# Rotary products taken straight from PSUM and added on GpSimd, one tile per step

## The chip, the core and the metric

The kernel runs on one core of one Trainium2 chip. The metric is the device time of one execution in microseconds. Five engines work side by side, each with its own instruction queue that it works off in order: TensorE (PE in the profile), VectorE (DVE), ScalarE (ACT), GpSimd (POOL) and SyncE (SP), which here only issues DMAs. They meet through semaphores.

## The reference, cut to what matters

Four sequences of 1024 tokens of width 128 go through causal attention with 8 heads of width 128, a layer norm, a gated feed-forward network and another layer norm, all in float32. What the change touches is the rotation of queries and keys:

```python
even, odd = jnp.split(x, 2, axis=-1)
return jnp.concatenate([even * cos - odd * sin, even * sin + odd * cos], axis=-1)
...
s = jnp.einsum('bihd,bjhd->bhij', q, k) / D_HEAD
s = s - INF_APPROX * mask          # mask is 1 where i < j
p = jax.nn.softmax(s, axis=-1)
```

## The kernel before, in words

Attention runs as 32 heads (4 sequences of 8), in pairs, in a loop whose body is written out. Matrix products are made from float32 numbers split into a high and a low float32r part, three products each (high by high, high by low, low by high). Head by head the work is a pipeline of eight steps, s = 0 to 7, one for each block of 128 query rows. In step s of the running head

- TensorE makes the scores of block s + 2 (blocks 0 and 1 of the next head in steps 6 and 7), then transposes the probabilities of block s, then projects tiles of the queries and keys of the next head, then values (in steps 4, 5, 6, 6 of the first head of a pair only), then pieces of the product of probabilities and values. Each is a call in `step` of the TensorE block, and nothing overtakes.
- VectorE takes the reciprocal of the row sums of block s + 1 (`inverse_sum`), the maximum of the scores of block s + 2 (`negative_max`), adds a head to the residual (steps 0 and 4), makes the low part of the transposed block s, and does its part of the rotation.
- ScalarE takes the exponential of block s + 1, makes the high part of a rotated tile, the high part of the transposed block, and in the kernel before the copy `proj`.
- GpSimd multiplies the probabilities of block s + 1 by the reciprocal sums (`normalize`, L720), then does its part of the rotation: `times_sin` (L725) and the low part `roped_low` (L732).

I write *norm(n)* for GpSimd's normalization of block n, *scores(n)* for TensorE's product of block n, and *low(j)* for `roped_low` of tile j.

A head has four tiles to rotate: 0 and 1 are the first 512 tokens of the queries and of the keys, 2 and 3 the second 512. The rotation needs the two halves of the 128 dimensions exchanged; that is a pair of DMAs from one SBUF tile to another, issued by SyncE. Before the change a tile goes through: projection (TensorE, into a PSUM bank), copy to `proj` (ScalarE), swap DMA, product with the sine (GpSimd, from SBUF), product with the cosine (VectorE, from PSUM), sum (VectorE), high part (ScalarE), low part (GpSimd). The tuples `QK_STEP` to `LOW_STEP` at the top say in which step of the running head each tile takes each of these; 8 means step 0 of the head after. Within a step each engine does them in the order in which its `step` function calls them.

What waits for the rotation is `scores`: it holds for

```python
wait_for(pe, rope_low, head, 1 if ib < 4 else 3)
```

so scores(0) of a head wait for low(1), and scores(4), in step 2 of the head itself, wait for low(3).

`plan_banks` gives PSUM banks to scores, transposes, projections and values by least recent use; it reads `QK_STEP`. The causal mask is added to the scores by a product of an identity and a 128x128 triangle, both bf16 before, between the first and second product of the diagonal half (L393).

Of the kernel before, what the change touches and what calls it, by code (L numbers as in the profile page):

```python
# [17 lines left out]
F32R = mybir.dt.float32r  # L18
# [9 lines left out]
P = 128  # L28
# [18 lines left out]
ROPE_TILES = [(0, 0), (1, 0), (0, 1), (1, 1)]  # L47


QK_STEP = (0, 0, 2, 2)  # L50
COS_STEP = (0, 0, 2, 2)
SIN_STEP = (1, 2, 3, 4)
SUM_STEP = (2, 3, 4, 6)
HIGH_STEP = (3, 4, 6, 8)
LOW_STEP = (3, 4, 6, 8)
V_STEP = (4, 5, 6, 6)
PV0_PIECES = {6: range(0, 2), 7: range(2, 4)}
PV1_PIECES = {1: range(0, 2), 2: range(2, 4), 3: range(4, 8)}
# [61 lines left out]
def attention(nc, ctx, sem, rT, ident, x_split, qk_split, v_split, xT, w_q, w_k, w_vT, w_o, rope_in, ident_in, mask_in,  # L120
# [3 lines left out]
        return where.enter_context(nc.sbuf_tensor(name, shape, dt))  # L124

    rope = sb("rope", [P, 2, T])
    ident_b = sb("ident_b", [P, P], BF16)
    mask_b = sb("mask_b", [P, P], BF16)
    w_stage = sb("w_stage", [P, 2, 4, P], F32R)
    wv_stage = sb("wv_stage", [P, 2, 2 * P], F32R)  # L130
    x_moving = sb("x_moving", [P, 2, 2, T], F32R)
    qk = sb("qk", [P, 2, 2, 2, T], F32R)
    proj = sb("proj", [P, 2, BANK])
    by_cos = sb("by_cos", [P, NQK, BANK])
    swapped = sb("swapped", [P, NQK, BANK])

# [43 lines left out]
    t_high = (sem("t_high"), NT)  # L180
    t_low = (sem("t_low"), NT)
    qk_projected = (sem("qk_projected"), NQK)
    proj_copied = (sem("proj_copied"), 4)
    cos_done = (sem("cos_done"), 4)
    sin_done = (sem("sin_done"), 4)
    rope_done = (sem("rope_done"), 4)
# [26 lines left out]
    def step_on(head, by):  # L213
        return head[0], head[1] + by
# [99 lines left out]
    with nc.Block() as block:  # L314
        @block.sync
        def _(sp):

            sp.dma_start(raw_w[:, 0], w_q).then_inc(qk_loaded, 16)
            sp.dma_start(raw_w[:, 1], w_k).then_inc(qk_loaded, 16)
            sp.dma_start(rope[:], rope_in).then_inc(consts_loaded, 16)  # L320
            sp.dma_start(mask_f[:], mask_in).then_inc(consts_loaded, 16)
            sp.dma_start(ident[:], ident_in).then_inc(consts_loaded, 16)
            for b in range(1, B):
                sp.dma_start(raw_x[:, b], xT[:, b * T:(b + 1) * T]).then_inc(x_loaded[b], 16)


            def stage_x_moving(b):

                wait_for_pair(sp, v_projected, PAIRS_OF * (b - 1) - 1, NV - 1)
                sp.dma_start(x_moving[:, b % 2].bitcast(F32), x_split[b - 2]).then_inc(x_moved, 16)  # L330

            def stage_pair(b, hp):

                pair = PAIRS_OF * b + hp
                dynamic = not isinstance(hp, int)
                first = isinstance(pair, int) and pair == 0

                def stage_for_values():
                    src = v_parts[:, :, :2 * P].bitcast(F32) if first else v_split[hp] if not dynamic else \
                        v_split[bass.ds(sp.snap(hp + 0), 1)].rearrange("o p k d -> p (o k) d")  # L340
                    wait_for_pair(sp, v_projected, pair - 1, NV - 1)
                    if first:
                        sp.wait_ge(vo_low, 1)
                    sp.dma_start(wv_stage[:].bitcast(F32), src).then_inc(wv_staged, 16)

                for q in range(2):
                    head = (pair, q)
                    src = qk_split[bass.ds(sp.snap(2 * hp + q), 1)].rearrange("o p k d -> p (o k) d") if dynamic else \
                        qk_split[2 * hp + q]
                    if not first:  # L350
                        wait_for(sp, qk_projected, step_on(head, -2), NQK - 1)
                        sp.dma_start(w_stage[:, q].bitcast(F32), src).then_inc(w_staged[q][0], 16)
                    if q == 0 and not first:
                        stage_for_values()
                    for j in range(NQK):
                        wait_for(sp, proj_copied, head, j)
                        for lo, hi in ((0, 64), (64, 0)):
                            sp.dma_start(swapped[lo:lo + 64, j], proj[hi:hi + 64, j % 2]).then_inc(
                                swap_done[j % 2][0], 16)
                    if q == 0 and first:  # L360
                        stage_for_values()

            stage_pair(0, 0)
            sp.wait_ge(w_saved, W_SAVED)
            with sp.Fori(1, PAIRS_OF) as hp:
                stage_pair(0, hp)
            sp.wait_ge(x_saved, X_SAVED)
            for base, src in zip(FFN_AT, ffn_weights):
                sp.dma_start(ffn_raw[:, base:base + src.shape[1]], src).then_inc(ffn_loaded, 16)
            for b in range(1, B):  # L370
                stage_pair(b, 0)
                if b < B - 1:
                    stage_x_moving(b + 1)
                with sp.Fori(1, PAIRS_OF) as hp:
                    stage_pair(b, hp)

        @block.tensor
        def _(pe):
            def scores(head, ib):
# [7 lines left out]
                for h in range(halves):  # L387
                    dst = score_ps[:, ib % 2, h, :half]
                    left = [a[:, ib * P:(ib + 1) * P] for a in q]
                    right = [a[:, h * half:(h + 1) * half] for a in k]  # L390
                    nc.tensor.matmul(dst, left[0], right[0], start=True, stop=False)  # L391
                    if h == halves - 1:
                        nc.tensor.matmul(dst[:, half - P:], ident_b[:], mask_b[:], start=False, stop=False)  # L393
                    nc.tensor.matmul(dst, left[0], right[1], start=False, stop=False)  # L394
                    last = nc.tensor.matmul(dst, left[1], right[0], start=False, stop=True)  # L395
                last.then_inc(scores_ready[0], 1)
# [86 lines left out]
        def _(act):  # L483
# [55 lines left out]
                        bank("t", head[1], nth)[:, :n_blocks * P].rearrange("p (j i) -> p j i", i=P),  # L539
                        ACT.Copy).then_inc(t_high[0], 1)  # L540

            def copy_projected(head, j):
                wait_for(act, qk_projected, head, j)
                old_head, old = earlier(head, j, 2, 4)
                wait_for_swap(act, old_head, old)
                wait_for(act, rope_low, step_on(head, -1), j)

                nc.scalar.activation(proj[:, j % 2], bank("qk", 1 if parity(head) else 2, j),  # L548
                                     ACT.Copy).then_inc(proj_copied[0], 1)

            def roped_high(head, j):
                which, c = ROPE_TILES[j]
                wait_for(act, rope_done, head, j)
# [12 lines left out]
            def step(head, s, b):  # L566
# [25 lines left out]
                for target, j in rope_tasks(head, s, QK_STEP):  # L592
                    copy_projected(target, j)
                for c in v_tasks(head, s):
                    values_high(head[0], c)

# [3 lines left out]
        def _(dve):  # L600
# [45 lines left out]
                        low, bank("t", head[1], nth)[:, :n_blocks * P].rearrange("p (j i) -> p j i", i=P),  # L646
                        high.bitcast(F32), ALU.subtract).then_inc(t_low[0], 1)

            def times_cos(head, j):
                c = ROPE_TILES[j][1]  # L650
                wait_for(dve, proj_copied, head, j)
                wait_for(dve, rope_done, step_on(head, -1), j)
                nc.vector.tensor_tensor(by_cos[:, j], bank("qk", 1 if parity(head) else 2, j),
                                        rope[:, 0, c * BANK:(c + 1) * BANK],
                                        ALU.mult).then_inc(cos_done[0], 1)

            def rope_sum(head, j):
                wait_for(dve, sin_done, head, j)
                wait_for(dve, cos_done, head, j)
                nc.vector.tensor_tensor(swapped[:, j], by_cos[:, j], swapped[:, j], ALU.add).then_inc(rope_done[0], 1)  # L660
# [19 lines left out]
            def step(head, s, b):  # L680
                if before_first(head) and s == 3:
                    dve.wait_ge(vo_high, 1)
                    nc.vector.tensor_tensor(v_parts[:, 1], vo_ps, v_parts[:, 0].bitcast(F32),
                                            ALU.subtract).then_inc(vo_low, 1)
                    nc.vector.tensor_copy(ident_b[:], ident[:])
                    nc.vector.tensor_copy(mask_b[:], mask_f[:]).then_inc(masks_ready, 1)
                if before_first(head) and s == 5:
                    for b in range(1, B):
                        low_of_x(b)
                if exists(step_on(head, (s + 1) // NI)):  # L690
                    inverse_sum(step_on(head, (s + 1) // NI), (s + 1) % NI)
                for target, j in rope_tasks(head, s, SUM_STEP):
                    rope_sum(target, j)
                if exists(step_on(head, (s + 2) // NI)):
                    negative_max(step_on(head, (s + 2) // NI), (s + 2) % NI)
                if s == ADD0_STEP:
# [2 lines left out]
                    add_head(step_on(head, -1), 1)  # L699
                if exists(head):  # L700
                    transposed_low(head, s)
                for target, j in rope_tasks(head, s, COS_STEP):
                    times_cos(target, j)
                for c in v_tasks(head, s):
                    values_low(head[0], c)

# [3 lines left out]
        def _(pool):  # L710
# [8 lines left out]
                p = probs[:, ib % 4, :(ib + 1) * P]  # L719
                nc.gpsimd.tensor_scalar(p, p, inv_sum[:, n:n + 1], 1.0, ALU.mult, ALU.mult).then_inc(probs_ready[0], 1)  # L720

            def times_sin(head, j):
                c = ROPE_TILES[j][1]
                wait_for_swap(pool, head, j)
                nc.gpsimd.tensor_tensor(swapped[:, j], swapped[:, j], rope[:, 1, c * BANK:(c + 1) * BANK],  # L725
                                        ALU.mult).then_inc(sin_done[0], 1)

            def roped_low(head, j):
                which, c = ROPE_TILES[j]
# [4 lines left out]
            def step(head, s, b):  # L734
                ahead = step_on(head, (s + 1) // NI)
                if exists(ahead):
                    normalize(ahead, (s + 1) % NI)
                for target, j in rope_tasks(head, s, SIN_STEP):
                    times_sin(target, j)
                for target, j in rope_tasks(head, s, LOW_STEP):  # L740
                    roped_low(target, j)

# [459 lines left out]
```

## Time and profile before

| | us |
|---|---|
| median of 3 runs (1081.2 to 1084.93) | 1084.09 |
| the profiled execution's own time | 1084.27 |
| its span | 1082.5 |
| TensorE busy | 1000.0 |
| VectorE busy | 852.7 |
| ScalarE busy | 657.0 |
| GpSimd busy | 584.8 |

Attention fills the span up to about 785 us, the feed-forward part the rest. The start of scores(0) of one head and of the next lie 22.83 to 25.01 us apart. In the trace a head can be recognised by its scores: the L391 product is 128 columns wide for block 0, 256, 384 and 512 for blocks 1 to 3, and twice 320, 384, 448 and 512 for blocks 4 to 7. In the stretch used below, the head that is running up to 407.95 us is the second of its pair (it projects no values), and the one running from there to 430.78 us is the first of the next pair (it does).

### The profile page before, as it was taken

To read this page: it belongs to the slowest core of one execution; us is meant where nothing else is said; L and a number is where in the kernel's file an instruction comes from. 1 tells how busy PE (TensorE), PEld (TensorE's weight loads), DVE (VectorE), ACT (ScalarE), POOL (GpSimd) and SP (SyncE) were. 2 spreads that over 40 slices of the span, in tenths; PEclk is the share of its full clock that TensorE was granted. 3 is DMA by queue.
4 is the path that set the end of the run, shared out by engine and by line. 5 is a ranking of instruction groups with operands and counts; after the bars stand their busy time and mean duration, and the time that the engine had idled before them with its cause. 6 is when DMAs were issued, how large, how long until landed. Compare 5 with 4: busy or idle time off the path is not lost. (4 is left out here: it accounts for less than half of the span.)

```text
span 1082.5 us, 20027 instructions
## 1 busy us (share of the span) xinstructions
PE 1000.0 (92%) x5648; PEld 829.6 (77%) x5648; DVE 852.7 (79%) x1803; ACT 657.0 (61%) x1383; POOL 584.8 (54%) x536
## 2 busy tenths in 40 slices
PE   2799999999999999999999999999929999999995
PEld 1588788878878888887888888787727878788784
DVE  4888888988878898897989888888755668486744
ACT  4577776777767777776767777677625252343531
POOL 3676777777767777777787776778450101000000
PEclk8899999999999999999999999999969999999998
DMA  7542223532222323222222223231020000000000
GB/s 247 166 137 60 63 63 87 156 88 59 59 60 67 78 58 88 59 61 67 68 67 58 50 59 73 59 80 42 1 79 1 1 1 21 0 19 0 1 20 20
DMA packets 33292, 66.16 MB, mean 61 GB/s; under 512 B 5456, under 2 KB 6992, under 8 KB 32208
## 3 DMA queue, kind: packets, MB, share of 16 engines
q1 hardware_dynamic: 30400, 58.62, 20.4%
q10 hardware_dynamic: 2832, 6.82, 1.7%
q8 instruction: 29, 0.48, 0.2%
q14 instruction: 31, 0.25, 0.1%
HBM read 24.26 MB, written 7.34 MB: 29 GB/s over the span
## 5 line engine op out<-in xcount | busy, mean ns | idle before, releaser
L720 POOL TENSOR_SCALAR probs<-probs,inv_sum 128x128 f32<-128x128 f32 (+7 forms) x256 | 236.2, 923 | 177.9 <-DVE inv_sum L635 177.9
L537 ACT ACTIVATE pT<-psum 128x512 fp32r<-128x512 f32 (+3 forms) x384 | 176.1, 490 | 129.8 <-PE psum L404 128.7
L311 PE MATMUL psum<-pT,vals 128*128 128x512 f32 (+3 forms) x1152 | 243.5, 351 | 1.6 <-DVE rT L678 1.6
L525 ACT ACTIVATE probs<-psum,neg_max 128x128 f32<-128x128 f32 (+7 forms) x256 | 190.5, 744 | 57.3 <-DVE neg_max L629 55.6
L645 DVE TENSOR_TENSOR pT<-psum,pT 128x512 fp32r<-128x512 f32 (+3 forms) x384 | 199.9, 547 | 15.1 <-ACT pT L537 12.0
L311 PEld LDWEIGHTS psum<-pT,vals 128*128 128x128 f32 x1152 | 188.9, 190 | 23.6 <-DVE pT L645 1.7
L629 DVE TENSOR_REDUCE neg_max<-psum 128x1 f32<-128x128 f32 (+7 forms) x256 | 190.4, 744 | 6.3 <-PE psum L395 6.3
L404 PE MATMUL psum<-ident,probs 128*128 128x128 f32 x1152 | 175.8, 278 | 15.0 <-POOL probs L720 7.6
L725 POOL TENSOR_TENSOR swapped<-swapped,rope 128x512 f32<-128x512 f32 x128 | 166.2, 1299 | 39.5 <-DMA swapped<-proj 38.6
L901 PE MATMUL ps<-hid,w 128*128 128x512 f32 x768 | 181.3, 396 | 0.0
L901 PEld LDWEIGHTS ps<-hid,w 128*128 128x128 f32 x768 | 143.7, 188 | 34.5
L732 POOL TENSOR_TENSOR qk<-swapped,qk 128x512 fp32r<-128x512 f32 x128 | 166.1, 1298 | 2.8 <-ACT qk L556 2.8
L404 PEld LDWEIGHTS psum<-ident,probs 128*128 128x128 f32 x1152 | 134.5, 141 | 42.1 <-DVE pT L645 13.1
L391 PE MATMUL psum<-qk 128*128 128x384 f32 (+5 forms) x384 | 136.7, 356 | 25.8 <-POOL qk L732 22.9
L660 DVE TENSOR_TENSOR swapped<-by_cos,swapped 128x512 f32<-128x512 f32 x128 | 123.1, 963 | 44.9 <-POOL swapped L725 44.9
L394 PE MATMUL psum<-qk 128*128 128x384 f32 (+5 forms) x384 | 151.3, 394 | 0.0
L395 PE MATMUL psum<-qk 128*128 128x384 f32 (+5 forms) x384 | 131.8, 343 | 0.0
L311 PE MATMUL psum<-x_moving,w_stage 128*128 128x512 f32 (+1 forms) x384 | 106.7, 414 | 9.9 <-DVEq L622 9.9
L995 ACT ACTIVATE value<-ps,scales 128x512 f32<-128x512 f32 x64 | 43.5, 690 | 96.9 <-PE ps L901 96.5
L391 PEld LDWEIGHTS psum<-qk 128*128 128x128 f32 x384 | 73.0, 190 | 36.0 <-issue 26.8
L1026 POOL COPY y<-y_norm 128x512 f32<-128x512 f32 (+1 forms) x8 | 5.2, 653 | 166.3 <-DVE y_norm L1083 166.3
L548 ACT ACTIVATE proj<-psum 128x512 f32<-128x512 f32 x128 | 75.2, 600 | 30.8 <-PE psum L311 26.1
(78 smaller groups left out, 1246.5 us busy)
## 6 DMA issues: line engine op xcount, KB each, us to landing
swapped<-proj SPq DMA_DIRECT2D x256, 128.0 KB, 2.3
w_stage<-qk_split SPq DMA_DIRECT2D x30, 256.0 KB, 2.7
wv_stage<-v_split SPq DMA_DIRECT2D x15, 256.0 KB, 2.6
x_split<-ffn_raw ACTq DMA_DIRECT2D x2, 1024.0 KB, 5.9
ffn_raw<-g SPq DMA_DIRECT2D x2, 1024.0 KB, 8.2
x_moving<-x_split SPq DMA_DIRECT2D x2, 1024.0 KB, 6.0
out<-y SPq DMA_DIRECT2D x4, 512.0 KB, 2.6
raw_x<-xT SPq DMA_DIRECT2D x3, 512.0 KB, 11.5
```

Source lines behind the costliest of these rows:

```text
L311: ins = nc.tensor.matmul(out_ap, left[a], right[b], start=first and i == 0, stop=last and i == 2)
L391: nc.tensor.matmul(dst, left[0], right[0], start=True, stop=False)
L394: nc.tensor.matmul(dst, left[0], right[1], start=False, stop=False)
L404: last = nc.tensor.transpose(bank("t", head[1], nth)[:, (jb % 4) * P:(jb % 4 + 1) * P], probs[:, ib % 4, jb * P:(jb + 1) * P], ident[:])
L525: nc.scalar.activation(probs[:, ib % 4, :width].rearrange("p (h c) -> p h c", h=halves), score_ps[:, ib % 2, :halves, :half], ACT.Exp, bia ...
L537: nc.scalar.activation(pT[chunk][:, 0, 4 * f:4 * f + n_blocks, (ib % 4) * P:(ib % 4 + 1) * P], bank("t", head[1], nth)[:, :n_blocks * P].r ...
L629: nc.vector.tensor_reduce(neg_max[:, n:n + 1], score_ps[:, ib % 2, :halves, :half], AX.XY, ALU.max, negate=True).then_inc(max_ready[0], 1)
L645: nc.vector.tensor_tensor(low, bank("t", head[1], nth)[:, :n_blocks * P].rearrange("p (j i) -> p j i", i=P), high.bitcast(F32), ALU.subtra ...
L720: nc.gpsimd.tensor_scalar(p, p, inv_sum[:, n:n + 1], 1.0, ALU.mult, ALU.mult).then_inc(probs_ready[0], 1)
L725: nc.gpsimd.tensor_tensor(swapped[:, j], swapped[:, j], rope[:, 1, c * BANK:(c + 1) * BANK], ALU.mult).then_inc(sin_done[0], 1)
L732: nc.gpsimd.tensor_tensor(low, swapped[:, j], high.bitcast(F32), ALU.subtract).then_inc(rope_low[0], 1)
L901: last = nc.tensor.matmul(ps[:, c, o], w_at(base, a, k * HID, o * P), hid[:, c, layer, b, k], start=k == 0 and i == 0, stop=k == HT - 1 an ...
```

## The change

The sine product moves from GpSimd, after the swap, to VectorE, before the swap, and reads the projection in PSUM; the copy on ScalarE is gone. The swap DMA carries the sine product instead of the projection, so the sine table changes its signs. GpSimd adds the two products in place of multiplying. Tiles are projected one per step, and the tuples move: tile j is projected in step j; low(0) to low(3) come in steps 4, 5, 8 and 9 instead of 3, 4, 6 and 8. Identity and mask become float32r.

```diff
-QK_STEP = (0, 0, 2, 2)
-COS_STEP = (0, 0, 2, 2)
-SIN_STEP = (1, 2, 3, 4)
-SUM_STEP = (2, 3, 4, 6)
-HIGH_STEP = (3, 4, 6, 8)
-LOW_STEP = (3, 4, 6, 8)
+QK_STEP = (0, 1, 2, 3)
+SUM_STEP = (2, 3, 6, 7)
+HIGH_STEP = (3, 4, 7, 8)
+LOW_STEP = (4, 5, 8, 9)
...
-    ident_b = sb("ident_b", [P, P], BF16)
-    mask_b = sb("mask_b", [P, P], BF16)
+    ident_r = sb("ident_r", [P, P], F32R)
+    mask_r = sb("mask_r", [P, P], F32R)
...
-                        wait_for(sp, proj_copied, head, j)
+                        wait_for(sp, sin_done, head, j)
...
-                            sp.dma_start(swapped[lo:lo + 64, j], proj[hi:hi + 64, j % 2]).then_inc(
+                            sp.dma_start(swapped[lo:lo + 64, j], by_sin[hi:hi + 64, j % 2]).then_inc(
...
-            def copy_projected(head, j):
-                wait_for(act, qk_projected, head, j)
...
-            def times_cos(head, j):
+            def rope_products(head, j):
                 c = ROPE_TILES[j][1]
-                wait_for(dve, proj_copied, head, j)
-                wait_for(dve, rope_done, step_on(head, -1), j)
-                nc.vector.tensor_tensor(by_cos[:, j], bank("qk", 1 if parity(head) else 2, j),
-                                        rope[:, 0, c * BANK:(c + 1) * BANK],
+                projected = bank("qk", 1 if parity(head) else 2, j)
+                old_head, old = earlier(head, j, 2, 4)
+                wait_for(dve, qk_projected, head, j)
+                wait_for_swap(dve, old_head, old)
+                wait_for(dve, rope_low, step_on(head, -1), j)
+                nc.vector.tensor_tensor(by_sin[:, j % 2], projected, rope[:, 1, c * BANK:(c + 1) * BANK],
+                                        ALU.mult).then_inc(sin_done[0], 1)
+                nc.vector.tensor_tensor(by_cos[:, j], projected, rope[:, 0, c * BANK:(c + 1) * BANK],
                                         ALU.mult).then_inc(cos_done[0], 1)
...
-                for target, j in rope_tasks(head, s, SUM_STEP):
-                    rope_sum(target, j)
                 if exists(step_on(head, (s + 2) // NI)):
                     negative_max(step_on(head, (s + 2) // NI), (s + 2) % NI)
...
-                for target, j in rope_tasks(head, s, COS_STEP):
-                    times_cos(target, j)
+                for target, j in rope_tasks(head, s, QK_STEP):
+                    rope_products(target, j)
...
-            def times_sin(head, j):
-                c = ROPE_TILES[j][1]
+            def rope_sum(head, j):
                 wait_for_swap(pool, head, j)
-                nc.gpsimd.tensor_tensor(swapped[:, j], swapped[:, j], rope[:, 1, c * BANK:(c + 1) * BANK],
-                                        ALU.mult).then_inc(sin_done[0], 1)
+                wait_for(pool, cos_done, head, j)
+                nc.gpsimd.tensor_tensor(swapped[:, j], by_cos[:, j], swapped[:, j], ALU.add).then_inc(rope_done[0], 1)
...
-                for target, j in rope_tasks(head, s, SIN_STEP):
-                    times_sin(target, j)
+                for target, j in rope_tasks(head, s, SUM_STEP):
+                    rope_sum(target, j)
                 for target, j in rope_tasks(head, s, LOW_STEP):
                     roped_low(target, j)
...
-    rope = np.stack([np.concatenate([cos, cos]), np.concatenate([-sin, sin])], axis=1).astype(np.float32)
+    rope = np.stack([np.concatenate([cos, cos]), np.concatenate([sin, -sin])], axis=1).astype(np.float32)
```

## Rows read from the trace of the kernel before

**Rows 1.** The page: busy us, share of the span and instructions of each engine.

```profile
PE 1000.0 (92%) x5648; PEld 829.6 (77%) x5648; DVE 852.7 (79%) x1803; ACT 657.0 (61%) x1383; POOL 584.8 (54%) x536
```

**Rows 2.** Busy us of each engine in 90 to 780 us; last three: clock, DMA share, GB/s.

```profile
90.00:780.00 690.00, 669.96 (x4118) 563.32 (x4116) 598.16 (x1172) 494.38 (x1113) 507.91 (x467) 1.00 0.27 67
```

**Rows 3.** Instruction groups by shape: busy us, mean ns of one | idle before them, releasers.

```profile
L725 POOL TENSOR_TENSOR swapped<-swapped,rope 128x512 f32<-128x512 f32 x128 | 166.2, 1299 | 39.5 <-DMA swapped<-proj 38.6 <-DVE inv_sum L635 0.8
L732 POOL TENSOR_TENSOR qk<-swapped,qk 128x512 fp32r<-128x512 f32 x128 | 166.1, 1298 | 2.8 <-ACT qk L556 2.8
...
L660 DVE TENSOR_TENSOR swapped<-by_cos,swapped 128x512 f32<-128x512 f32 x128 | 123.1, 963 | 44.9 <-POOL swapped L725 44.9
...
L653 DVE TENSOR_TENSOR by_cos<-psum,rope 128x512 f32<-128x512 f32 x128 | 83.2, 684 | 6.5 <-ACT proj L548 4.3 <-DMA ident<-ident_in 1.1
...
L548 ACT ACTIVATE proj<-psum 128x512 f32<-128x512 f32 x128 | 75.2, 600 | 30.8 <-PE psum L311 26.1 <-DMA swapped<-proj 2.5 <-issue 0.3
```

**Rows 4.** Timeline of TensorE, 402 to 432 us: start, duration, instruction, [idle <-releaser].

```profile
402.55 0.42 PE L391 MATMUL psum<-qk 128*128 128x448 f32 x1
...
407.95 0.32 PE L391 MATMUL psum<-qk 128*128 128x128 f32 x1 [0.70 <-POOL qk L732]
...
408.87 0.98 PE L404 MATMUL psum<-ident,probs 128*128 128x128 f32 x7 [0.30 <-POOL probs L720]
...
412.91 0.39 PE L391 MATMUL psum<-qk 128*128 128x384 f32 x1
...
417.52 0.31 PE L391 MATMUL psum<-qk 128*128 128x320 f32 x1
...
417.96 0.31 PE L391 MATMUL psum<-qk 128*128 128x320 f32 x1
...
418.52 0.49 PE L404 MATMUL psum<-ident,probs 128*128 128x128 f32 x3
...
430.78 0.22 PE L391 MATMUL psum<-qk 128*128 128x128 f32 x1
...
431.25 0.44 PE L404 MATMUL psum<-ident,probs 128*128 128x128 f32 x2
```

**Rows 5.** Timeline of GpSimd in the same stretch.

```profile
406.55 1.27 POOL L732 TENSOR_TENSOR qk<-swapped,qk 128x512 fp32r<-128x512 f32 x1
407.79 1.02 POOL L720 TENSOR_SCALAR probs<-probs,inv_sum 128x896 f32<-128x896 f32 x1
...
416.90 0.59 POOL L720 TENSOR_SCALAR probs<-probs,inv_sum 128x384 f32<-128x384 f32 x1 [0.94 <-DVE inv_sum L635]
...
430.18 1.01 POOL L720 TENSOR_SCALAR probs<-probs,inv_sum 128x896 f32<-128x896 f32 x1
```

**Rows 6.** Timeline of VectorE in the same stretch.

```profile
402.85 1.71 DVE L660 TENSOR_TENSOR swapped<-by_cos,swapped 128x512 f32<-128x512 f32 x1
...
406.88 0.15 DVE L635 RECIPROCAL inv_sum<-row_sum 128x1 f32<-128x1 f32 x1
...
415.25 1.38 DVE L653 TENSOR_TENSOR by_cos<-psum,rope 128x512 f32<-128x512 f32 x2
416.54 0.15 DVE L635 RECIPROCAL inv_sum<-row_sum 128x1 f32<-128x1 f32 x1
...
429.83 0.14 DVE L635 RECIPROCAL inv_sum<-row_sum 128x1 f32<-128x1 f32 x1
```

**Rows 7.** The page's DMA issues: count, KB each, us from issue to landing.

```profile
swapped<-proj SPq DMA_DIRECT2D x256, 128.0 KB, 2.3
```

**Rows 8.** Weight loads by shape, 300 to 700 us, columns as in Rows 3.

```profile
L391 PEld LDWEIGHTS psum<-qk 128*128 128x128 f32 x204 | 38.5, 189 | 11.2 <-issue 6.4 <-POOL qk L732 1.7
...
L393 PEld LDWEIGHTS psum<-mask_b,ident_b 128*128 128x128 bf16 x136 | 13.0, 96 | 20.8 <-issue 15.7
```

**Rows 9.** Windows around the one fall of the clock between 100 and 780 us.

```profile
310.20:313.66 3.46, 1.66 (x9) 0.76 (x7) 3.46 (x6) 1.97 (x4) 3.46 (x4) 1.00 0.00 0
313.66:317.07 3.41, 3.41 (x14) 3.04 (x15) 2.83 (x8) 3.16 (x7) 2.41 (x3) 0.50 0.00 0
```

More of the change, by code:

```diff
@@ L132, in attention @@
     qk = sb("qk", [P, 2, 2, 2, T], F32R)
-    proj = sb("proj", [P, 2, BANK])
+    by_sin = sb("by_sin", [P, 2, BANK])
     by_cos = sb("by_cos", [P, NQK, BANK])
@@ L182, in attention @@
     qk_projected = (sem("qk_projected"), NQK)
-    proj_copied = (sem("proj_copied"), 4)
     cos_done = (sem("cos_done"), 4)
@@ L392, in scores @@
                     if h == halves - 1:
-                        nc.tensor.matmul(dst[:, half - P:], ident_b[:], mask_b[:], start=False, stop=False)
+                        nc.tensor.matmul(dst[:, half - P:], ident_r[:], mask_r[:], start=False, stop=False)
                     nc.tensor.matmul(dst, left[0], right[1], start=False, stop=False)
@@ L540, in transposed_high @@
                         ACT.Copy).then_inc(t_high[0], 1)
-            def copy_projected(head, j):
-                wait_for(act, qk_projected, head, j)
[L544 to L549, printed above, removed]
             def roped_high(head, j):
@@ L591, in step @@
                     transposed_high(head, s)
-                for target, j in rope_tasks(head, s, QK_STEP):
-                    copy_projected(target, j)
                 for c in v_tasks(head, s):
@@ L647, in transposed_low @@
                         high.bitcast(F32), ALU.subtract).then_inc(t_low[0], 1)
-            def times_cos(head, j):
+            def rope_products(head, j):
                 c = ROPE_TILES[j][1]
-                wait_for(dve, proj_copied, head, j)
-                wait_for(dve, rope_done, step_on(head, -1), j)
-                nc.vector.tensor_tensor(by_cos[:, j], bank("qk", 1 if parity(head) else 2, j),
-                                        rope[:, 0, c * BANK:(c + 1) * BANK],
+                projected = bank("qk", 1 if parity(head) else 2, j)
[6 more added lines that the diff above has]
+                nc.vector.tensor_tensor(by_cos[:, j], projected, rope[:, 0, c * BANK:(c + 1) * BANK],
                                         ALU.mult).then_inc(cos_done[0], 1)
[L657 to L660, printed above, removed]
             def values_low(pair, nth):
@@ L684, in step @@
                                             ALU.subtract).then_inc(vo_low, 1)
-                    nc.vector.tensor_copy(ident_b[:], ident[:])
-                    nc.vector.tensor_copy(mask_b[:], mask_f[:]).then_inc(masks_ready, 1)
+                    nc.vector.tensor_copy(ident_r[:], ident[:])
+                    nc.vector.tensor_copy(mask_r[:], mask_f[:]).then_inc(masks_ready, 1)
                 if before_first(head) and s == 5:
```

## The prediction, made before the changed kernel was run

> **What bounds the kernel now.** I began with the page: TensorE is busy for 92% of the span, VectorE 79%, ScalarE 61%, GpSimd 54% [rows 1]. That average holds the feed-forward part, where GpSimd does almost nothing and which the change does not touch, so I read the attention part by itself: TensorE 670 of 690 us, VectorE 598, GpSimd 508, ScalarE 494 [rows 2]. TensorE sets the pace, and what it loses it loses at waits of tenths of a microsecond. The groups show what the rotation costs the others: the instructions that the change moves are 128 each of the ScalarE copy, the cosine product, the sum on VectorE and the sine product on GpSimd [rows 3]. Busy time of three engines that TensorE does not wait for is worth nothing by itself. So I went to the timelines of one head of each kind and asked at every semaphore that TensorE waits for how early it comes. The rotation meets TensorE in two places: scores(0) of the next head wait for low(1), and scores(4) wait for low(3).
>
> Today scores(0) are late only in the head without value projections: they start at 407.95, behind a low(1) that ends at 406.55 + 1.27 = 407.82 [rows 4, 5]. So a GpSimd result reaches TensorE 0.13 us after its end. Right after it the transposes wait for norm(6) and start at 408.87. In the head with values, TensorE arrives later and scores(0) start at 430.78 without a wait [rows 4].
>
> **What goes, and is worth little.** ScalarE loses 128 copies of 0.600 = 75 us; VectorE loses 128 sums of 0.963 = 123 us with 44.9 us of waiting for GpSimd, and gains 128 sine products, which I price like the cosine products from PSUM, 0.684 each = 88 us [rows 3]. GpSimd trades a two-operand product for a two-operand sum: 1.30 for each stays (bounds: 0.96, what VectorE's sum takes, and 1.71, the longest such row; I take 1.30, the same engine's). None of this is work of TensorE. Where it reaches TensorE is through the softmax chain: the sum of tile 2 stood ahead of the maximum of block 6 at 402.85 and took 1.71 us [rows 6]. With it gone, the maximum can start when scores(6) are done, at an estimated 404.1 (from 402.55 six products of 448 columns, by the 0.44 us that three of 320 take in rows 4, with the mask, and the run-out of the last one), in place of 404.5, but ScalarE and the transposes behind it then bind, and I give the reciprocal of block 6 only 0.2 us.
>
> The row of that sum has a cause behind it: 1.71 us beside a GpSimd instruction against a mean of 0.963 [rows 3, 6]. By the Trainium skill, "SBUF — State Buffer", section "Who interferes with whom", VectorE instructions with two SBUF inputs and GpSimd instructions share a port pair under an exclusive lock. The trace agrees; it says that the new products, which read PSUM and one SBUF tile, go free of it, as the 0.684 of the cosine product does. It changes no term of the sum below.
>
> **What is added, one: low(3) behind norm(2).** Before, low(3) is the second rotation task of step 0, right behind norm(1). Now low(2) stands there, and low(3) is in step 1 behind norm(2), in the same queue. When can norm(2) start? At 416.90, 0.21 us after the reciprocal of block 2 at 416.54 + 0.15. That reciprocal stands in VectorE's queue behind two rotation products of step 0, at 415.25, 1.38 us [rows 5, 6]. The new order has two products there as well (sine and cosine of tile 0, in place of cosine of tiles 0 and 1), so the freed ScalarE helps nothing and norm(2) starts at 416.90 as before. norm(2) takes 0.59, less 0.03 by which such spans overlap in the rows: 417.46. low(3) 1.29: 418.75. 0.13 to TensorE: 418.88. And TensorE reaches scores(4) at 417.52 [rows 4]. Steps 0 and 1 together keep their length: they had tiles 0 and 1 in step 0, now one in each, so 412.91 to 417.52 stands. The wait is 1.36 us. It comes in both kinds of heads, since no values are projected in steps 0 to 3: 31 x 1.36 = 42.2 us. Bounds: 0 if the reciprocal of block 2 came 1.4 us sooner, 31 x 2.0 if the sum or high part of tile 3 is late too.
>
> **Two: low(1) behind norm(6).** low(1) moves from step 4 to step 5, behind norm(6). norm(6) hangs on the reciprocal of block 6.
>
> - Head without values: reciprocal at 406.88 + 0.15 less 0.2 = 406.83; norm(6) at 407.04 (+0.21); 0.99 later 408.03; low(1) 1.28: 409.31; TensorE 409.44. Before: 407.95. But the 0.44 us that the transposes waited for norm(6) goes, since norm(6) is now ahead: with 0.47 from scores(0) to the transposes (431.25 - 430.78) [rows 4] they start at 409.91 against 408.87. Net 1.04.
> - Head with values: reciprocal at 429.83 + 0.14 less 0.2; norm(6) at 429.98 instead of 430.18; 430.97; low(1) to 432.26; TensorE 432.39 against 430.78, which had no wait: 1.61 us [rows 4, 5, 6].
>
> 15 heads of the first kind and 16 of the second run ahead of another head: 15.6 + 25.8 = 41.4 us. Bounds: nothing below 0; at most 31 x 2.7 if norm(5) and low(0), ahead of it, push norm(6) too. By the same adding up they are done about 1 us before norm(6) can start.
>
> The two waits do not share a cause, so they add: from scores(6) to scores(0) is one chain, from scores(2) to scores(4) another, and a late start of either is handed on unchanged.
>
> **What else moves, at no cost.** The sums: sum(0) and sum(1) have the swap behind them with 2.3 us of landing [rows 7] against more than a step; SyncE's loads for the next head are queued behind the swap of tile 3, one step later, with five steps left. sum(2) and sum(3) stand in steps 6 and 7 on GpSimd ahead of norm(0) and norm(1): scores(2) start 4.96 us after scores(0) [rows 4], and the transposes of block 0 later still; until then GpSimd owes norm(7), a sum, norm(0) and a sum, 2.6 us for the sums and an estimated 2.0 for the two norms, by the 1.02 of norm(6) [rows 5]. That cover is thin, 0.5 us or somewhat more; where it is gone, the rest of it lands on the path. VectorE gets two products in steps 1 and 3 and is ahead in steps 2 to 4. The PSUM bank of a projection is freed by the second product as now.
>
> **The mask.** On TensorE a masked half of 320 columns takes 418.52 - 417.96 = 0.56 us, an unmasked one 0.44: the bf16 product costs 0.12 [rows 4]. A float32r one of 128 columns is bounded by 0.06 (128 columns at the rate of the 320 column product, 0.147 us, of which its share is 0.059) and by 0.19, its weight load laid bare [rows 8]; the transposes, of 128 columns with loads of their own, run at (0.98 - 0.27)/6 = 0.12 in rows 4, the nearest, so the exchange is worth 0; bounds -15 and +18 us over 256.
>
> The Trainium skill, "TensorE: Matmul & The Clock Gate", section "Weight-path perf modes — Fast Weight Load (FWL) and DoubleRow", speaks against this edit: a full 128-column load is fast only when its type is not float32. The load rows agree, 96 ns against 189 [rows 8]; by the rule alone the sum would be up to 0.093 x 256 = 24 us longer. But bf16 loads show idle before them, 20.8 us, where float32 loads start beneath the product before, so I do not add it.
>
> **The clock.** Once TensorE was busy for only 1.66 of 3.46 us, and the granted clock then was 0.50 (1.2 of 2.4 GHz) for 3.41 us [rows 9]. Heads without values now have a wait of about 2.5 us before scores(0) (from about 407.0 to 409.44). A fall costs half of 3.41 = 1.7, less what of it lies in the wait itself, which I put at 0.5 by judgement: 1.2. I expect it in about half of the 15, a guess between that one fall and one in each: 8 x 1.2 = 9.6 us. Bounds 0 and 31 x 1.7 = 53.
>
> **Sum.** The profiled execution took 1084.3 (span 1082.5 and 1.8 around it; the median of the runs, 1084.1, is the same for this purpose). 1084.3 + 42.2 + 41.4 + 9.6 = 1177.5, so 1177.
>
> **Rivals.**
> - *Only one of the two waits lasts.* The freed ScalarE and VectorE bring norm(2) or norm(6) early enough. For it: three engines get lighter. Against: the queue ahead of the reciprocal of block 2 is as long as before. 1084 + 42 = 1126, up to 1150 with falls of the clock. Chance 0.13.
> - *The clock falls in nearly every head.* For it: 1.4 and 1.6 to 2.5 us of waits in each head, and rows 9. Against: the clock's mean over the 690 us is 1.00 [rows 2], so the other heads of the first kind, with their waits, show next to none. 1167.9 + 31 x 1.2 to 1.7 = 1205 to 1221. Chance 0.12.
> - *Faster: the relief wins.* VectorE no longer waits 44.9 us in all for GpSimd ahead of maxima, and the maxima lead to everything. If norm(6) started 2.5 us and norm(2) 1.4 us sooner than I have them, both waits would vanish, and with them today's: 0.70 and 0.30 us in each of 15 heads [rows 4]: 1084.3 - 15 = 1069. It decides from the point at which low(1) ends before TensorE is through with the transposes of step 5. Against: the exponential of block 6 cannot start before its scores, and the reciprocal of the block lies 4.3 us behind their start [rows 4, 6]. Chance 0.06.
> - *It changes nothing*: shorter chains just pay for the later slots, 1084. Chance 0.03.
>
> **How the numbers follow.** Both waits as worked out, with some falls: 0.66, own range 1155 to 1200. The predicted time is 1177. The range 1130 to 1206 leaves out the lower part of the first rival, most of the second and all with no loss. What a measurement can tell from no change is about 0.3%: faster 0.06, same 0.03, slower 0.91.
>
> **What would show it.** In the profile after, idle of TensorE before the first L391 product of 320 columns, released by the low part on GpSimd, about 1.4 us in each head; the same before the 128-column one, 1.6 to 2.5 us; no wait of the transposes behind it; GpSimd with norm(2), low and norm(6), low back to back; ScalarE 75 us and VectorE 35 us less busy. It is wrong if scores(4) start without a wait, or if the spacing of heads stays near today's 23.5 us instead of about 26.2.

## The result, and the profile after

The changed kernel takes 1184.49 us (median of 4 runs, 1181.92 to 1187.21) against 1082.64 us (4 runs) for the kernel before: ratio 1.0966, 95% interval 1.0941 to 1.0992 (the two medians by themselves give 1.0941, the low end of it). I forecast 1177 and a range of 1130 to 1206. The profiled execution took 1184.64 us, its span is 1182.8.

The page after, engine shares as in [rows 1]: ScalarE is 62 us less busy, VectorE 25 and GpSimd 47, and TensorE, which was given no work, is busy for 37 us more.

```profile
PE 1037.0 (88%) x5648; PEld 890.5 (75%) x5648; DVE 827.5 (70%) x1803; ACT 594.5 (50%) x1255; POOL 537.6 (45%) x536
```

The window of 90 to 780 us after, to be held against [rows 2]: TensorE's busy time fell from 670 to 614 of 690 us, and the granted clock, the third number from the end, from 1.00 to 0.95.

```profile
90.00:780.00 690.00, 613.51 (x3582) 540.23 (x3582) 501.25 (x1020) 382.64 (x869) 408.82 (x410) 0.95 0.24 61
```

TensorE's groups by shape after, from 60 to 880 us (busy, mean | idle just before them, who ended it). The first score product is L388 now (L391 before), the low part L714 (L732), the normalization L703 (L720), the transposes L401 (L404).

```profile
L401 PE MATMUL psum<-ident,probs 128*128 128x128 f32 x1099 | 172.4, 286 | 5.1 <-DVE pT L631 4.0 <-POOL probs L703 1.0
...
L388 PE MATMUL psum<-qk 128*128 128x320 f32 x62 | 22.3, 359 | 27.0 <-POOL qk L714 27.0
...
L388 PE MATMUL psum<-qk 128*128 128x128 f32 x30 | 10.1, 337 | 59.1 <-POOL qk L714 59.1
```

The same view of the kernel before:

```profile
L404 PE MATMUL psum<-ident,probs 128*128 128x128 f32 x1115 | 170.0, 278 | 12.2 <-POOL probs L720 6.8 <-DVE pT L645 5.1
...
L391 PE MATMUL psum<-qk 128*128 128x128 f32 x30 | 8.2, 274 | 10.1 <-POOL qk L732 10.1
```

The 128-column product is scores(0), the 320-column one scores(4): idle before them rose from 10.1 to 59.1 us and from nothing to 27.0, all released by GpSimd's low part; the transposes lost 7 us of theirs. (The window leaves out the first two heads. Rows count from the modelled end of the product before. Counted from when the next product could have started, about 0.16 us sooner, the waits of 31 heads are 65.5 and 31.9 us, against 12.5 and 0; the expectations below use these.)

One head without values after, TensorE from scores(6) on: scores(6), the transposes of block 5, scores(0), the transposes of block 6, and in the next head scores(2), the transpose of block 0, scores(3), scores(4).

```profile
445.12 0.41 PE L388 MATMUL psum<-qk 128*128 128x448 f32 x1
...
448.55 0.93 PE L401 MATMUL psum<-ident,probs 128*128 128x128 f32 x6
451.83 0.32 PE L388 MATMUL psum<-qk 128*128 128x128 f32 x1 [2.35 <-POOL qk L714]
...
452.33 1.48 PE L401 MATMUL psum<-ident,probs 128*128 128x128 f32 x7
...
457.91 0.39 PE L388 MATMUL psum<-qk 128*128 128x384 f32 x1
...
459.10 0.30 PE L401 MATMUL psum<-ident,probs 128*128 128x128 f32 x1 [0.34 <-DVE pT L631]
...
459.99 0.39 PE L388 MATMUL psum<-qk 128*128 128x512 f32 x1
...
463.65 0.42 PE L388 MATMUL psum<-qk 128*128 128x320 f32 x1 [0.39 <-POOL qk L714]
```

GpSimd in the same stretch: norm(6) and low(1), then norm(2) and low(3), each pair back to back and each waiting for VectorE's reciprocal.

```profile
449.46 1.01 POOL L703 TENSOR_SCALAR probs<-probs,inv_sum 128x896 f32<-128x896 f32 x1 [1.76 <-DVE inv_sum L621]
450.44 1.27 POOL L714 TENSOR_TENSOR qk<-swapped,qk 128x512 fp32r<-128x512 f32 x1
...
461.76 0.59 POOL L703 TENSOR_SCALAR probs<-probs,inv_sum 128x384 f32<-128x384 f32 x1 [0.80 <-DVE inv_sum L621]
462.31 1.29 POOL L714 TENSOR_TENSOR qk<-swapped,qk 128x512 fp32r<-128x512 f32 x1
```

VectorE's part of the second chain: two products, then the reciprocal.

```profile
460.19 0.69 DVE L642 TENSOR_TENSOR by_sin<-psum,rope 128x512 f32<-128x512 f32 x1
460.80 0.68 DVE L644 TENSOR_TENSOR by_cos<-psum,rope 128x512 f32<-128x512 f32 x1
461.40 0.15 DVE L621 RECIPROCAL inv_sum<-row_sum 128x1 f32<-128x1 f32 x1
```

From scores(6) to scores(0) it is 6.71 us (5.40 before [rows 4]; I had worked out 6.89), from scores(2) to scores(4) 5.74 (4.61 before; worked out 5.97). The low parts end 0.12 and 0.05 us before TensorE starts. This is one head: over all 31, the end of low(1) lies 0.13 us ahead of scores(0) in 22 and about 0.05 in 9, that of low(3) 0.22 us or more ahead of scores(4) in 22 and about 0.05 in 9, and from scores(2) to scores(4) it is mostly 6.2 us in the first head of a pair and 5.9 in the second.

The windows of that wait and of what follows: TensorE busy for 1.05 us of 3.40, then a granted clock of 0.51, so about 1.2 of 2.4 GHz.

```profile
449.20:452.60 3.40, 1.05 (x9) 0.81 (x9) 2.34 (x6) 2.06 (x4) 2.82 (x3) 1.00 0.00 0
452.60:456.10 3.50, 3.50 (x15) 3.21 (x14) 1.45 (x4) 1.95 (x5) 2.63 (x4) 0.51 0.00 0
```

Between the ramp at the start and the end of attention the trace's clock records show 21 stretches of 3.41 us at the half clock, against 2 before, one of them that of [rows 9]. They are why TensorE is busy for longer. 19 of the 20 places where they start lie 0.04 to 1.6 us behind the start of a scores(0), that is, after its wait. They come in runs: 13 of the 19 distances between these places are 27.3 us, and from the second head on a head with one fall is 26.7 to 27.8 us long, one without 25.7 to 26.2. So the falls tend to follow one another from head to head.

### The profile page after: what moved, and what is told of

It is laid out like the page before. It is cut to its first block and busy times, and to the rows that moved or that the text cites. A ratio compares the mean times of both kernels' runs of the same rounds, so it can differ in the third digit from the quotient of the medians.

```text
span 1182.8 us, 19698 instructions
## 1 busy us (share of the span) xinstructions
PE 1037.0 (88%) x5648; PEld 890.5 (75%) x5648; DVE 827.5 (70%) x1803; ACT 594.5 (50%) x1255; POOL 537.6 (45%) x536
## 5 line engine op out<-in xcount | busy, mean ns | idle before, releaser
L703 POOL TENSOR_SCALAR probs<-probs,inv_sum 128x128 f32<-128x128 f32 (+7 forms) x256 | 191.1, 746 | 350.6 <-DVE inv_sum L621 350.6
L308 PE MATMUL psum<-pT,vals 128*128 128x512 f32 (+3 forms) x1152 | 251.5, 361 | 1.7 <-DVE rT L663 1.6
L388 PE MATMUL psum<-qk 128*128 128x384 f32 (+5 forms) x384 | 143.0, 372 | 96.9 <-POOL qk L714 93.7
L308 PEld LDWEIGHTS psum<-pT,vals 128*128 128x128 f32 x1152 | 203.2, 199 | 31.7 <-DVE pT L631 1.7
L401 PE MATMUL psum<-ident,probs 128*128 128x128 f32 x1152 | 180.4, 286 | 5.6 <-DVE pT L631 4.0
L708 POOL TENSOR_TENSOR swapped<-by_cos,swapped 128x512 f32<-128x512 f32 x128 | 165.5, 1293 | 16.2 <-DMA swapped<-by_sin 16.1
L388 PEld LDWEIGHTS psum<-qk 128*128 128x128 f32 x384 | 74.3, 193 | 122.6 <-issue 59.5
L714 POOL TENSOR_TENSOR qk<-swapped,qk 128x512 fp32r<-128x512 f32 x128 | 163.8, 1280 | 0.0
L401 PEld LDWEIGHTS psum<-ident,probs 128*128 128x128 f32 x1152 | 143.4, 146 | 25.8 <-DVE pT L631 6.2
L391 PE MATMUL psum<-qk 128*128 128x384 f32 (+5 forms) x384 | 145.3, 378 | 0.0
L308 PE MATMUL psum<-x_moving,w_stage 128*128 128x512 f32 (+1 forms) x384 | 123.3, 431 | 10.2 <-DVEq L608 10.1
L642 DVE TENSOR_TENSOR by_sin<-psum,rope 128x512 f32<-128x512 f32 x128 | 87.3, 682 | 7.4 <-PE psum L308 6.1
L644 DVE TENSOR_TENSOR by_cos<-psum,rope 128x512 f32<-128x512 f32 x128 | 87.1, 680 | 0.0
L544 ACT ACTIVATE qk<-swapped 128x512 fp32r<-128x512 f32 x128 | 80.3, 627 | 3.9 <-POOL swapped L708 3.5
```

What stands on the lines that cost most here:

```text
L308: ins = nc.tensor.matmul(out_ap, left[a], right[b], start=first and i == 0, stop=last and i == 2)
L401: last = nc.tensor.transpose(bank("t", head[1], nth)[:, (jb % 4) * P:(jb % 4 + 1) * P], probs[:, ib % 4, jb * P:(jb + 1) * P], ident[:])
L708: nc.gpsimd.tensor_tensor(swapped[:, j], by_cos[:, j], swapped[:, j], ALU.add).then_inc(rope_done[0], 1)
L714: nc.gpsimd.tensor_tensor(low, swapped[:, j], high.bitcast(F32), ALU.subtract).then_inc(rope_low[0], 1)
```

## The experiments

All but e11 are edits of the changed kernel. "Before" took 1079.1 to 1079.9 us on the three chips of these runs; the changed kernel was not run again there, so I compare with 1184.5 and leave 0.3% between the two sets open. Waits are given from the time at which TensorE was ready; falls are stretches of 3.41 us at half clock in attention, counted in the profiled execution alone.

### e1: low(3) back to step 0

```diff
-LOW_STEP = (4, 5, 8, 9)
+LOW_STEP = (4, 5, 8, 8)
```

> Only the low part of tile 3 goes back from step 1 to step 0 of the running head (LOW_STEP 4, 5, 8, 8), behind norm(1) and not norm(2). Theory of the queue place: TensorE's wait before scores(4), 31.9 us in all in the changed kernel, is gone; the wait before scores(0) stays at 65 us; since a fall of the clock is no longer taken up in part by the wait before scores(4), some 5 to 10 us come back: 1184.5 - 32 + 7 = about 1160. Rival, the rotation's data are late (two products on VectorE, then the swap, then the sum in step 7): the wait before scores(4) stays at 20 us or more and the time is 1175 to 1185.

1136.6 us, ratio to before 1.0524 (1.0500 to 1.0547). The groups of TensorE, 60 to 880 us:

```profile
L388 PE MATMUL psum<-qk 128*128 128x320 f32 x60 | 19.0, 317 | 0.4 <-POOL qk L714 0.4
L388 PE MATMUL psum<-qk 128*128 128x128 f32 x30 | 9.8, 327 | 59.2 <-POOL qk L714 59.2
```

The wait before scores(4) is gone, that before scores(0) is untouched: the queue place was the cause, the data were there. I missed the time by 23 us, since falls did not come back but went from 21 to 14. 32 us of wait and 7 falls at 1.6 us (from e3) make 43 of the 48 us.

### e2: low(1) back to step 4

```diff
-LOW_STEP = (4, 5, 8, 9)
+LOW_STEP = (4, 4, 8, 9)
```

> Only the low part of tile 1 goes back from step 5 to step 4 (LOW_STEP 4, 4, 8, 9), ahead of norm(6). Theory of the queue place: the wait before scores(0) falls from 65 us to under 10, the transposes of block 6 wait for norm(6) again in the heads without values (about 0.5 us in each of 15), and nearly all 3.41 us falls of the clock go (21 in the changed kernel). 1184.5 - 60 + 7 - 15 = about 1117. Rival, data late: sum or high part of tile 1 come too late for step 4 and GpSimd stands still behind them; wait before scores(0) stays over 30 us, time over 1150. Rival, the falls of the clock cost nothing because they lie in waits: 1130 to 1135.

1120.0 us, ratio 1.0370 (1.0350 to 1.0390), 2 falls.

```profile
L401 PE MATMUL psum<-ident,probs 128*128 128x128 f32 x1113 | 168.0, 277 | 31.0 <-DVE pT L631 19.0 <-POOL probs L703 11.3
L388 PE MATMUL psum<-qk 128*128 128x320 f32 x62 | 22.1, 356 | 26.2 <-POOL qk L714 26.2
L388 PE MATMUL psum<-qk 128*128 128x128 f32 x30 | 7.9, 265 | 0.0
```

The time came as expected, but not by my sum. The wait before scores(0) went altogether, with 19 falls, which is some 95 us; 26 us came back as waits of the transposes, which are 31.0 us now, against 5.1 in the changed kernel; 19.0 of the 31.0 are for VectorE's low part of a transposed block, against 4.0. That was a wait that I had not foreseen, and the wait before scores(0) had covered most of it; e7 to e10 turn on it.

### e3: work for TensorE in the wait

```diff
             def scores(head, ib):
+                if ib == 0 and exists(step_on(head, -1)):
+                    pair, off = head if ("s", head[1], ib) in USES else (head[0] - 1, head[1] + 2)
+                    wait_for_banks(pe, pair, "s", off, ib)
+                    old_k = qk[:, 1 - parity(head), 1, 0]
+                    for _ in range(6):
+                        nc.tensor.matmul(score_ps[:, 0, 0, :BANK], old_k[:, :P], old_k[:, :BANK], start=True, stop=True)
```

> The changed kernel, with six products of 512 columns on TensorE ahead of the wait for low(1) in scores(0) of every head but the first; their result is overwritten, so they are work added in a wait (1.3 us of 1.8 to 2.5). Theory that the falls of the clock follow this wait and cost about 1 us each: the 21 falls become 5 or fewer, the waits for low(1) by the clock of the semaphore stay, and the time goes down by 10 to 25 us although 31 x 1.3 = 40 us of work are added: 1160 to 1175. Rival, the falls lie in waits and cost nothing: 1184 within 4 us. Rival, the products do not fit the wait: over 1190.

1150.3 us, ratio 1.0653 (1.0632 to 1.0673): 34 us less time with 40 us more work. No fall is left, and the 90 to 780 us window has a clock of 1.00:

```profile
90.00:780.00 690.00, 649.29 (x3918) 563.91 (x3918) 523.96 (x1068) 400.62 (x912) 426.70 (x427) 1.00 0.25 64
```

So 34.2 us over 21 falls is 1.6 us each, close to the whole 1.7 of half a stretch: they hardly lie in waits. The gain was above my 10 to 25.

### e4: the mask in bf16

```diff
-    ident_r = sb("ident_r", [P, P], F32R)
-    mask_r = sb("mask_r", [P, P], F32R)
+    ident_r = sb("ident_r", [P, P], BF16)
+    mask_r = sb("mask_r", [P, P], BF16)
```

> The changed kernel with identity and mask of the causal mask in bf16 again. My estimate was that the float32r form costs the same (0.12 us a product): 1184 within 3 us. If the slower weight load of float32r (197 ns against 96) lay on the path, the time would fall by up to 24 us, to 1160 to 1175; if the bf16 form is the slower one, whose load does not start beneath the product before, it would rise by 2 to 6 us.

1170.6 us, ratio 1.0851 (1.0818 to 1.0884): 14 us less, where I expected none. The waits are nearly the same (59.1 and 26.4 us in the rows); the falls are 11 instead of 21, and 10 x 1.6 = 16 us. Taken alone this looks like the weight load of the float32r form, for which I had written 1160 to 1175. e8 and e11 say no.

### e5: VectorE's products of tile 0 behind the reciprocal of block 2

```diff
+PROD_STEP = (1, 1, 2, 3)
...
-                for target, j in rope_tasks(head, s, QK_STEP):
+                for target, j in rope_tasks(head, s, PROD_STEP):
                     rope_products(target, j)
```

> The changed kernel with its steps of the low parts untouched; only VectorE's two products of tile 0 are made at the end of step 1, behind the reciprocal of block 2, in place of step 0. Theory of the queue: norm(2) starts late because these two products (1.38 us) stand ahead of the reciprocal; with them behind it, norm(2) and low(3) come about 1.4 us sooner and the wait before scores(4) (31.9 us in all) goes to under 3, as it did when low(3) was moved. Time about 1137, as with low(3) moved, 1130 to 1145. Rival: low(3) waits for something else (exponential, sum of tile 3): wait before scores(4) over 20 us, time 1175 to 1185. Rival: the tile's later swap makes sum(0) late, and what is won is lost at block 3: 1150 to 1170.

1152.2 us, ratio 1.0674 (1.0653 to 1.0696). The wait before scores(4) fell from 31.9 to 7.8 us, not under 3: the two products do hold up the reciprocal, as I had read in [rows 6], and without them 0.5 us are left in every second head. There GpSimd's own queue is what holds: low(2), norm(2) and low(3) run without a pause, and scores(4) start at 423.66, behind the last of them.

```profile
420.33 1.28 POOL L715 TENSOR_TENSOR qk<-swapped,qk 128x512 fp32r<-128x512 f32 x1
421.59 0.59 POOL L704 TENSOR_SCALAR probs<-probs,inv_sum 128x384 f32<-128x384 f32 x1
422.14 1.30 POOL L715 TENSOR_TENSOR qk<-swapped,qk 128x512 fp32r<-128x512 f32 x1
```

The other heads show no wait: at the transpose of block 0, of which more at e7, TensorE lost 0.7 us (from scores(2) to scores(3) 2.19 against 1.49 us), so it comes later. With 18 falls where e1 has 14, most of the 15.6 us to e1 is accounted for (7 + 4 x 1.6 = 13.4).

### e6: the engines of the change in the steps of the kernel before

```diff
-QK_STEP = (0, 1, 2, 3)
-SUM_STEP = (2, 3, 6, 7)
-HIGH_STEP = (3, 4, 7, 8)
-LOW_STEP = (4, 5, 8, 9)
+QK_STEP = (0, 0, 2, 2)
+SUM_STEP = (1, 2, 3, 4)
+HIGH_STEP = (3, 4, 6, 8)
+LOW_STEP = (3, 4, 6, 8)
...   with identity and mask in bf16
```

> The engines of the changed kernel in the steps of the kernel before: projections in steps 0, 0, 2, 2, GpSimd's sum where its sine product stood (1, 2, 3, 4), high and low parts in 3, 4, 6, 8, mask in bf16. What is left of the change is then the move of work alone: no copy on ScalarE, sine product on VectorE from PSUM, sum on GpSimd. Theory that all of the loss is in the steps: not slower than before, and up to 20 us faster, since the maximum of blocks 4 to 6 no longer stands behind a sum that waits for GpSimd: 1060 to 1080 against 1079. Rival, that the work itself sits worse on VectorE and GpSimd: 1090 or more.

1073.1 us, ratio 0.9936 (0.9910 to 0.9961): 0.6% faster than before. The move of work between engines is a small gain, and the loss is in the steps. (The bf16 mask came back as well; e11 has its price without falls.)

### e7 and e8: steps that keep low(1) and low(3) ahead

```diff
-SUM_STEP = (2, 3, 6, 7)
-HIGH_STEP = (3, 4, 7, 8)
-LOW_STEP = (4, 5, 8, 9)
+SUM_STEP = (2, 3, 5, 6)
+HIGH_STEP = (3, 4, 6, 7)
+LOW_STEP = (3, 4, 7, 8)
```

> The changed kernel, float32r mask and projections in steps 0 to 3 kept, with sums in 2, 3, 5, 6, high parts in 3, 4, 6, 7 and low parts in 3, 4, 7, 8: low(1) is ahead of norm(6) and low(3) ahead of norm(2), and each step of GpSimd from 2 on has at most two rotation tasks. Theory: both waits and all the falls of the clock go, 1184.5 - 97 - 34 plus 5 to 15 for smaller waits behind norm(5) and norm(6): 1058 to 1070, faster than before (1079) by about 1%. Rival: TensorE is held at the same place by the same queue of GpSimd as in the kernel before: 1075 to 1085.

> The same steps with the mask in bf16. If the mask's form acts only through the falls of the clock (10 falls fewer with bf16 in the changed kernel, 14 us), and there are none here, the two take the same time within 2 us. If the form costs by itself, 256 products show 2 us or more for each 0.01 us.

e7: 1083.7 us, ratio 1.0037 (1.0021 to 1.0053); e8, the same with e4's edit: 1084.6, ratio 1.0046 (1.0031 to 1.0060). No falls in either, and no difference: the mask's form has no price of its own. But my 1058 to 1070 was wrong, and the time fits my rival while its cause does not: behind the first head TensorE never waits for a low part. It waits here, behind scores(2) of every second head, 19.0 us in all:

```profile
361.44 0.33 PE L401 MATMUL psum<-ident,probs 128*128 128x128 f32 x1 [1.23 <-DVE pT L631]
```

`plan_banks` starts with empty counts, though its body repeats. With one projection per step it gives the transpose of block 0 bank 4, which the last transpose of block 7 of the head before took two uses back, so TensorE waits until VectorE has read that.

### e9 and e10: another start of the bank plan

```diff
-    last = dict.fromkeys(range(PV_BANK), 0)
+    last = dict.fromkeys(range(PV_BANK), 0) | {4: 0, 5: 0.1, 6: 0.2}
```

> The kernel with the other steps (sums 2, 3, 5, 6; high 3, 4, 6, 7; low 3, 4, 7, 8), float32r mask, with another start of the bank plan (banks 4, 5, 6 tried in that order). The plan counts from the first use of a pair of heads and does not see that its last use comes before its first: with one projection per step the transpose of block 0 of an even head got the bank of the last transpose of block 7 before it, two uses back, and TensorE waited for its low part, 1.3 to 1.7 us in 15 heads. Theory: that wait and some of the 0.3 us ahead of it go, 1083.7 less 20 to 28: 1055 to 1064, faster than the kernel before (1079) by 1.4 to 2.2%. Rival, the wait only covers the next one (norm(0) or scores(4)): 1075 to 1084.

> The changed kernel with that start of the bank plan alone. There TensorE waited about 0.7 us at the same transpose, in the chain from scores(2) to scores(4) that ends in a wait for low(3) anyway. Theory: the transposes of block 0 no longer wait, the wait before scores(4) of even heads grows from 0.9 to about 1.3 us, as in odd heads, and the time stays at 1184.5 within 5 us. Rival, the bank's wait was part of the loss by itself: 1170 to 1176.

e9, e7 with this line: 1068.6 us, ratio 0.9890 (0.9865 to 0.9914), the lowest of all (its interval just touches that of e6) and faster than both kernels of the case, though short of my 1055 to 1064. In the transposes' group the 19.0 us for VectorE are gone and the 11 us for norms stay:

```profile
L401 PE MATMUL psum<-ident,probs 128*128 128x128 f32 x1113 | 167.5, 277 | 13.7 <-POOL probs L703 11.6
```

e10, the changed kernel with this line: 1180.8 us, ratio 1.0926 (1.0899 to 1.0953), 23 falls. As expected, the wait only moves: scores(4) now wait 1.3 us in both kinds of heads (38 us in all), and scores(2) to scores(4) take 5.89 us in both. (The view puts 11 of these waits, 12.4 of 33.2 us, down to `by_cos`, which ends 0.15 us ahead of scores(4). By the plan their bank comes free with tile 0, whose product is done about two us sooner; the low part ends 0.24 us ahead, as it does, with 0.22, where the view names it.)

### e11: the kernel before with a float32r mask

```diff
-    ident_b = sb("ident_b", [P, P], BF16)
-    mask_b = sb("mask_b", [P, P], BF16)
+    ident_b = sb("ident_b", [P, P], F32R)
+    mask_b = sb("mask_b", [P, P], F32R)
```

> The kernel before with the float32r mask alone. My estimate from slots of TensorE: the same within 0.3% (1079 within 3 us), since it has nearly no falls of the clock through which the form could act. If the weight load lay on the path: up to 24 us slower; if the bf16 load's late start is what costs: 2 to 6 us faster.

1079.6 us, ratio 0.9995 (0.9979 to 1.0011): no change, with 2 falls as before.

## Why the prediction came out as it did

- **low(1) behind norm(6)**, 41.4 us: right in mechanism, somewhat too large. The wait itself is what I had worked out or more (2.35 and 1.62 us in the rows, 0.16 more from when TensorE was ready). What counts is what it replaced. From scores(6) of a head to scores(1) of the next it is 8.34 us before and 9.22 after where the running head has no values, and 9.94 and 11.26 where it has, in typical heads without a fall: 0.88 and 1.32 us more against my 1.04 and 1.61, 34 us over the 15 and 16 heads. I had taken off the wait for norm(6) in the first kind of head alone; the transposes of block 5 had been waiting in both, for VectorE, and that time was lost before as well (in heads with values it is 3.22 us from scores(7) to scores(0) before, and 2.89 in e6, where the sum is off VectorE and scores(0) do not wait either). e2 shows the cause.
- **low(3) behind norm(2)**, 42.2 us: right in mechanism, and in size for the chain. From scores(2) to scores(4) the 31 heads took 142.4 us before and 184.0 after, 41.6 more. The wait before scores(4) is only 31.9 us of them. I had said that the PSUM bank of a projection "is freed by the second product as now" and stopped there; spreading the projections had also re-dealt the other banks, and a wait at the transpose of block 0 took the place of a part of this one in every second head (scores(3) come 2.08 us behind scores(2) in the lines above, 1.49 in e10). With other banks (e10) the wait before scores(4) is 38 us. The time hardly notices, since one chain holds both. e1 and e5 show the cause, at the two ends of the chain.
- **The clock**, 9.6 us: the term that was most wrong in size. I put it at 8 falls of 1.2 us; there were 21, in heads of both kinds, at 1.6 us (e3), 34 us. The 0.5 us that I took off as lying in the wait was a guess and wrong: with one exception they begin once TensorE works again. The share of heads was a guess too, from a single fall [rows 9], and nothing in the trace of before could have given it; the bounds, 0 and 53, held it.
- **The mask**, 0: right for the product itself (e8, e11), wrong as a whole, since in the changed kernel the float32r form comes with 10 more falls, 14 us (e4). The Trainium skill's rule in "TensorE: Matmul & The Clock Gate", section "Weight-path perf modes — Fast Weight Load (FWL) and DoubleRow", whose price I did not add, is borne out in the load (197 ns against 96) and not in the time. How the form brings on falls stays open; no run tells whether it is the form or any small shift of the heads that would do it.
- **The other engines' relief**, 0 as a first step: e6 has it at 6 us by itself. ScalarE and VectorE were to be 75 and 35 us less busy and are 62 and 25; their instructions took 80 and 33 us less in sum, but the page counts spans that overlap once.

The terms as measured, 34 + 42 + 34 = 110 us, are over the 100.3 by which the span grew. Of the rest 3.6 come back at the start, where scores(0) of the first head begin at 25.6 us in place of 29.2. Some 9 more are time that single heads of the kernel before lost between scores(6) and scores(1), over the typical ones (its two falls are part of it), and that the new wait takes up; about 3 us were added behind scores(4). That the sum came out near 1177 is in part luck: the first term was 7 too large, the third 24 too small, and the 10 us that came back were not in the sum.

## What to carry to other kernels

When a task moves to a later slot of an engine's queue, price it by what stands ahead of it there and by who waits at the other end; the engine's lower busy share says nothing. Waits of 1.5 to 2.5 us on TensorE cost half as much again by the clock here (34 us on 65.5), so look at the granted clock of the stretches behind each new wait. If the order of work feeds a plan that hands out buffers, print the plan before and after, and go through the loop once more from its end to its start.

## What the runs showed of the hardware that I had not expected

GpSimd's normalization, which was not touched, became shorter. Three of its groups, those of 1024, 768 and 512 columns, 90 to 750 us, in the kernel before:

```profile
L720 POOL TENSOR_SCALAR probs<-probs,inv_sum 128x1024 f32<-128x1024 f32 x28 | 39.3, 1402 | 39.9 <-DVE inv_sum L635 39.9
L720 POOL TENSOR_SCALAR probs<-probs,inv_sum 128x768 f32<-128x768 f32 x28 | 37.7, 1346 | 0.0
L720 POOL TENSOR_SCALAR probs<-probs,inv_sum 128x512 f32<-128x512 f32 x29 | 34.0, 1172 | 0.0
```

and in the changed kernel:

```profile
L703 POOL TENSOR_SCALAR probs<-probs,inv_sum 128x1024 f32<-128x1024 f32 x25 | 28.0, 1120 | 12.0 <-DVE inv_sum L621 12.0
...
L703 POOL TENSOR_SCALAR probs<-probs,inv_sum 128x768 f32<-128x768 f32 x25 | 22.7, 907 | 46.7 <-DVE inv_sum L621 46.7
...
L703 POOL TENSOR_SCALAR probs<-probs,inv_sum 128x512 f32<-128x512 f32 x24 | 16.6, 692 | 8.9 <-DVE inv_sum L621 8.9
```

1402, 1346 and 1172 ns became 1120, 907 and 692, and the 1053 of 640 columns became 801. In the kernel before, a sum on VectorE overlapped every one of these four in time. The blocks of 896 and 384 columns, beside which no sum ran, kept 1014 and 587. So the contention that I had read off VectorE's sum of 1.71 us held up GpSimd as well, and the whole group went from 236.2 to 191.1 us of busy time. By the Trainium skill, "SBUF — State Buffer", section "Who interferes with whom", the shared port pair is an exclusive lock, and the order of issue decides which of the two is held up. By that rule both sides could gain, and the rows agree. I had used it for VectorE alone. In e6 the same durations (1124, 910, 695) stand beside a gain of 0.6% in time.
